# Ten subtractions of a graph layer on VectorE, put earlier in its list

## What is computed

```python
HW = h @ W
s = HW @ a[:512, 0];  t = HW @ a[512:, 0]
e = leaky_relu(s[row] + t[col], 0.2)             # row = src, col = dst
att = softmax of e over the edges of each row
agg = segment_sum(att[:, None] * h[col], row)
basis = _b_splines(agg, grid)                    # 8 cubic bases
out = silu(agg) @ base_w.T + einsum('nip,oip->no', basis, spline_w)
x = _layernorm(x + out)
```

## Time and profile before

| | us |
|---|---|
| median of 3 runs | 442.68 |
| lowest, highest | 442.21, 443.82 |
| the profiled execution | 445.38 |
| its span, first to last instruction | 443.6 |
| TensorE busy | 403.9 |
| VectorE busy | 367.4 |
| ScalarE busy | 272.4 |
| GpSimd (POOL) busy | 33.1 |

### The profile page before, as it was taken

How to read it: one execution, slowest core, us unless ns; L and a number is a source line. 1 busy time by engine, 2 the same in 40 slices (tenths; PEclk the granted TensorE clock), 3 DMA queues, 4 the chain that set the end, 5 groups by cost and what they waited for, 6 DMA issues and landing times.

```text
span 443.6 us, 5222 instructions
## 1 busy us (share of the span) xinstructions
PE 403.9 (91%) x1881; PEld 309.6 (70%) x1881; DVE 367.4 (83%) x457; ACT 272.4 (61%) x299; POOL 33.1 (7%) x162
## 2 busy tenths in 40 slices
PE   3999984494999999959999999989999999999994
PEld 0435653383888888838888888868877777777782
DVE  7968998787978852599996999898999989389965
ACT  7535673633566447687749676749676786647322
POOL 5100000100000000100011011010101101011000
PEclk9999999598899999987999999999999999999998
DMA  8970000600000000853453544513133167284303
GB/s 271 373 170 1 1 0 0 191 0 1 0 1 0 1 1 1 261 190 99 139 180 117 178 150 136 142 47 96 51 93 92 50 191 197 88 288 135 96 0 113
DMA packets 23452, 45.91 MB, mean 103 GB/s; under 512 B 1831, under 2 KB 2043, under 8 KB 23427
## 3 DMA queue, kind: packets, MB, share of 16 engines
q0 software_dynamic: 11088, 21.44, 17.4%
q1 hardware_dynamic: 12338, 24.14, 17.1%
HBM read 43.02 MB, written 2.56 MB: 103 GB/s over the span
## 4 chain that ended last, share of the span: by engine, by line
issue 44%; PE 42%; DVE 7%; DMA 3%; POOL 2%; ACT 0%; DVEq 0%; POOLq 0%
PE PS L1115 33%; PE PS L1010 5%; DMA wh<-in_splT 3%; POOL wh L373 2%; DVE still L413 2%; PE PS L986 2%; DVE oh L393 1%; DVE xl L501 1%; PE PS L965 1%; DMA ei<-in_edges 1%; DVE wl L592 1%; DVE v L702 0%; DVE v L698 0%; DVE v L696 0%; ACT s L905 0%
## 5 line engine op out<-in xcount | busy, mean ns | idle before, releaser
L1115 PE MATMUL PS<-wh,s 128*128 128x512 f32 (+1 forms) x720 | 226.5, 395 | 6.9 <-issue 5.5
L1115 PEld LDWEIGHTS PS<-wh,s 128*128 128x128 f32 (+1 forms) x720 | 134.6, 187 | 40.5 <-issue 5.9
L1115 PE MATMUL PS<-wl,s 128*128 128x512 f32 (+1 forms) x360 | 142.1, 395 | 0.0
L905 ACT ACTIVATE s<-v 128x1280 fp32r<-128x1280 f32 (+1 forms) x32 | 40.0, 1250 | 73.3 <-DVE v L702 65.0
L1115 PEld LDWEIGHTS PS<-wl,s 128*128 128x128 f32 (+1 forms) x360 | 67.4, 187 | 15.7
L1010 PE MATMUL PS<-oh,still 128*128 128x320 bf16 x304 | 46.0, 307 | 10.0 <-DVE still L413 8.0
L1010 PEld LDWEIGHTS PS<-oh,still 128*128 128x128 bf16 x304 | 29.0, 100 | 29.9 <-DVE still L413 10.5
L702 DVE SCALAR_TENSOR_TENSOR v<-v,v 128x1280 f32<-128x1280 f32 (+1 forms) x32 | 46.7, 1461 | 3.7 <-DVE v L698 0.5
L696 DVE SCALAR_TENSOR_TENSOR v<-v,v 128x1280 f32<-128x1280 f32 (+1 forms) x32 | 46.5, 1454 | 3.8 <-ACT v L890 3.8
L712 DVE SCALAR_TENSOR_TENSOR s<-v,s 128x1280 fp32r<-128x1280 f32 (+1 forms) x32 | 46.5, 1454 | 1.3 <-ACT s L905 1.3
L698 DVE SCALAR_TENSOR_TENSOR v<-v,v 128x1280 f32<-128x1280 f32 (+1 forms) x32 | 46.5, 1453 | 0.0
(11 more groups left out here) (125 smaller groups left out, 376.1 us busy)
## 6 DMA issues: line engine op xcount, KB each, us to landing
wh<-in_splT POOLq DMA_DIRECT2D x32, 512.0 KB, 4.4
wring<-in_splT SPq DMA_DIRECT2D x22, 512.0 KB, 3.9
xt<-in_xT SPq DMA_DIRECT2D x1, 2500.0 KB, 11.5
xn<-in_x SPq DMA_DIRECT2D x1, 2304.0 KB
xh<-in_x POOLq DMA_DIRECT2D x1, 2304.0 KB, 13.4
out<-xr SPq DMA_DIRECT2D x9, 256.0 KB
wh<-in_baseT POOLq DMA_DIRECT2D x4, 512.0 KB, 4.5
xr<-in_x SPq DMA_DIRECT2D x1, 1280.0 KB
```

Source lines behind the costliest of these rows:

```text
L905: e.activation(parts(sh, u), bufs(u)[0], ACT.Relu).then_inc(s_shi, 1)
L1115: m = e.matmul(PS[0:rows(w), w % 8, :], sx[:, ic, tl * 128:tl * 128 + rows(w)], wx[:, ic, :], start=first and n == 0, stop=last and n == 2)
```

## The change

`x_low(0)` to `x_low(9)` stand behind the one-hots of windows 15, 17, 19, ..., 33 in VectorE's list, and no longer behind 32, 34, 36, 38 and 39. `NT` is 10. Nothing else is touched; `x_low` itself, its waits included, is as it was.

```diff
--- before.py
+++ after.py
@@ -545,13 +545,11 @@
                     left_table()
                 if w == 25:
                     left_sizes()
-                if w >= 32 and w % 2 == 0:
-                    x_low((w - 32) // 2)
+                if 15 <= w < 15 + 2 * NT and w % 2:
+                    x_low((w - 15) // 2)
                 if w == SIZES_AT:
                     e.wait_ge(s_rest, RESTS)
                     windows = loaded(e, r_size, 0, 1, 1, NR + 1)[0]
-            for w in range(4, NT):
-                x_low(w)
 
 
             e.wait_ge(s_hole, ND)
```

## The result

The changed kernel takes 451.17 us in the median of 6 runs (448.69 to 451.77), the kernel before takes 442.70 (442.21 to 443.82, 6 runs). The ratio is 1.0174, with a 95% interval from 1.0144 to 1.0204: 1.7%, or 7.7 us (6.4 to 9.0), slower. The profiled execution took 450.74 us, with a span of 448.9.

The account below looks back on a forecast made before the run. VectorE's list, without free time from 41 us on, was taken as the bound of the counts; 3.61 - 0.78 + 3.35 + 0.60 = +6.78 us on the median of 442.68 gave 449.5 us, range 445.5 to 452.

Parts of the forecast that it names:

- The bound: First stage, the counts: VectorE has no free time from 41 us on, so each microsecond added moves its end as much.
- The six: Six subtractions moved ahead of window 39's one-hots in a list without gaps: 6 x 0.602 = +3.61 us.
- Free time behind window 15: VectorE's waits at windows 18 and 19, 0.61 + 0.17 us, are all filled by moved subtractions: -0.78 us.
- The wait carried along: x_low(0), behind window 15's one-hots, waits for s_sr at 3 from 34.65 until 38.00 us: +3.35 us.
- The last evacuation: s_hole comes 3.04 us after window 39's one-hots, against 2.44 before, no longer hidden by the tail: +0.60 us.
- Into the loop: From s_hole to one_moving 1.17 us as before: 0, with at most -0.8 us possible.
- rival 4: TensorE's clock level falls in the last windows, 21 matmuls at double time: +9.8 us, 452.5 us; chance 0.05.
- (1): The wait at x_low(0) costs nothing, xT being read before VectorE arrives: +3.43 us, 446.1 us; chance 0.05.
- (2): All ten subtractions hide in VectorE's waits of the first half: -1.8 us, 440.9 us; chance 0.03.
- (3): TensorE's half-clock stretches in later stages: both missed, +2.2 us, 444.9 us; one missed, +4 to +5; chance 0.1.
- Rival 5: The change doesn't act, as something else releases greatest: +0, 442.7 us; chance 0.01.
- Signs: Last Z near 80.3 us, one_moving near 81.5; wrong if the loop starts by 81 us and the end doesn't follow.

Follow-up runs that it names:

- all_tail: The control with all ten subtractions behind window 39's one-hots; loop start 0.00 us against the control, ratio 0.9988 to the kernel before.
- twice: The control with all ten subtractions behind window 39 and made twice over; loop start +6.02 us against the control, ratio 1.0138 to the kernel before.
- wait15: The control with only a wait for s_sr at 3 added behind window 15's one-hots; loop start +2.22 us, ratio 1.0048 to the kernel before.
- place14: The control with xl's memory traded, four subtractions behind window 14's one-hots and six behind window 39; loop start -2.11 us, ratio 0.9949 to the kernel before.
- gap4: The control with six subtractions behind window 39 and four in the next stage, around p_low(0)'s second part; loop start -2.12 us, ratio 0.9936 to the kernel before.
- place15: The changed kernel with xl's memory traded so nothing there waits for s_sr; loop start +2.75 us against the control, ratio 1.0054 to the kernel before.
- after_again: The changed kernel with the control's 15-bit cut in the loop; loop start +6.23 us against the control, ratio 1.0160 to the kernel before.
- control: The kernel before, with the number the loop's waits ask for cut to 15 bits by one more register operation; ratio 1.0012 to the kernel before.
- pool: The control with all ten subtractions on POOL, behind its loads of xh; loop start +2.93 us against the control, ratio 1.0071 to the kernel before.

## Why the prediction was right

- **The bound.** VectorE's list, full from 41 us on: right. all_tail (0.00), twice (+6.02 for ten subtractions of 0.602) and wait15 show it three ways, and place14 and gap4 a fourth: a shorter list brings the loop forward.
- **The six, +3.61.** Right: the step from one subtraction to the next is 0.60 us here too.
- **Free time behind window 15, -0.78.** Too small. The list from the first instruction behind the wait to the end of window 39's one-hots is 76.30 - 37.42 = 38.88 us; before it was 71.08 - 34.65 = 36.43 us, with six subtractions less (3.61). So 1.16 us of waiting was taken up. The prediction counted the brackets; they count from the end of an instruction's duration, which reaches some 0.08 us into the next step, and the smallest gaps have none (46.72 to 46.76 us in the kernel before). From start to start, the waits at windows 18 and 19 were 0.70 and 0.24 us.
- **The wait carried along, +3.35.** 3.49 us from start to start, shown also by place15 (3.49). The 0.14 us more is the way from TensorE's end (37.28) to VectorE's start (37.42), which the step took as nothing. In wait15 the same way is 0.03 us (36.87 to 36.90), so it is not a fixed cost. Alone the wait costs 2.22 us (wait15), because the 1.16 us of free time take up part of it. In the changed kernel the subtractions would have taken those up anyway, so there all of it counts.
- **The last evacuation, +0.60.** 79.34 - 76.30 = 3.04 us, as predicted.
- **Into the loop, 0.** It was -0.30, inside the stated bounds (-0.8 to 0). The sequencer did not wait for the tail, as the step took it; but it was through 0.3 us before the tail's last subtraction, and `one_moving` waited for that. The prediction read the tail as covering the way into the loop "nearly to the nanosecond"; it was 0.3 us longer than what it covered.
- **Sum.** 3.61 - 1.16 + 3.49 + 0.60 - 0.30 = 6.24 us, and 6.24 was measured. These terms are read from the rows that also give the 6.24, so the sum has to close; that they are costs of their own is shown by the experiments (place15: the same without 3.49; wait15: 3.38 - 1.16). The predicted 6.78 was 0.5 too high: the free time was taken as too small and the entry as too dear, the wait a little too cheap.
- **The time.** The predicted 449.5 us is 1.7 below the measured 451.17, though the sum at the loop was 0.5 too high: 442.7 + 6.24 is 448.9. The result lies in the upper part of the range, which was there for rival 4, and rival 4 did not happen. That the range holds it is in part luck.
- **The rivals.** The wait costs something, and most of the change (1); the ten did not hide (2), though place14 shows that four would have, one window earlier. The stretches at half clock were neither missed (3) nor added to (4): TensorE worked 60% of the time from 50 to 60 us at full clock. There is a third such stretch, which the prediction did not list: behind the loop the granted clock was 0.50 from 80 to 85 us and 0.70 from 85 to 90, and with the change 0.50 from 85 to 90 and 0.67 from 90 to 95. It too is shifted, at about the same length. Rival 5 falls with POOL's wait, which grew by 5.6 us.
- **Signs.** The last mask and the loop came at 79.3 and 80.2 us, before the 80.3 and 81.5 foretold: 0.72 us of it is the earlier first half of this execution, the rest the terms above. The loop did start by 81 us, but the sign of being wrong asked also that the end should not follow, and it followed.

**What stays open.** 6.24 us is 1.41% of 442.7, just under the lower end of the first comparison (1.44%), and inside that of after_again (1.30 to 1.91%; against the control 6.6 us). From `greatest` to the end single profiles of all these kernels lie between 364.4 and 367.6 us, in no order that follows the change. Whether the timed runs of the changed kernel hold another half or whole microsecond, and where, the runs do not tell.

## What to carry to other kernels

Before work is moved into "free" time, ask on which side of the wait the free time lies, and what waits the moved step brings with it: here 3 us of it lay one instruction ahead of the chosen place, and a wait for a shared buffer, long satisfied at the old place, cost 3.5 us at the new one. Work behind the last item of a stage is free as long as it is shorter than the time until that item has passed through the other engines (here 3.9 us); only what exceeds this is worth moving. And count idle time from start to start, as brackets leave out small gaps.

## What the runs showed of the hardware

- A subtraction of 128 by 512 numbers took VectorE 0.67 us and POOL, beside VectorE's comparisons, 1.26 to 19.98 us (median 1.71), with some of VectorE's own instructions longer by 0.4 to 1.1 us (pool). I had expected POOL to be free help while it stood idle.
- Entering the loop whose bounds come from memory took VectorE 0.87 us from the end of the last mask to the first instruction, 0.38 us of it the load (changed kernel).
- A waiting VectorE started 0.14 us (changed kernel) and 0.03 us (wait15) behind the end of the TensorE instruction that released it; the profile's ends of matmuls are modelled.
